# Graph sums of four blocks by row gathers on GpSimd, GpSimd's arithmetic moved to VectorE and DMA, main part unrolled

## The reference

```python
xn = _layernorm(x)
# graph part
h = xn * rsqrt(max(deg_out, 1))[:, None]
agg = segment_sum(h[src], dst, num_segments=N)
g = relu((agg * rsqrt(max(deg_in, 1))[:, None]) @ W + b)
g = g / max(norm(g), 1e-12)
# linear attention, 8 heads of 64, no softmax
dots = einsum('bnd,bnhe', instance_norm(k), instance_norm(v))
mix = ((q @ dots) / N) @ w_out.T + b_out
x = x + g + mix
# mixture of 8 experts, each token to its best one, with a capacity
return x + ffn(_layernorm(x))
```

## Time and profile before

| | before |
|---|---|
| median of 3 runs | 1471.17 us (1469.41 to 1475.35) |
| span of the profiled execution | 1429.1 us |
| that execution's own time | not listed; its span is 42.1 us below the median |
| PE busy | 1337.7 us (94%) |
| DVE busy | 1248.9 us (87%) |
| ACT busy | 962.9 us (67%) |
| POOL busy | 648.8 us (45%) |

### The profile page before, as it was taken

The page is one execution under the profiler, slowest core; times in us unless marked ns, Lnnn a source line. Parts: engine busy times, 40 slices in busy tenths (PEclk is TensorE's granted clock), DMA queues, the critical chain, the costliest instruction groups (busy, mean ns, idle before and its releaser), DMA issues. The chain is left out here.

```text
span 1429.1 us, 43152 instructions
## 1 busy us (share of the span) xinstructions
PE 1337.7 (94%) x14715; PEld 1128.4 (79%) x14717; DVE 1248.9 (87%) x2315; ACT 962.9 (67%) x2239; POOL 648.8 (45%) x645
## 2 busy tenths in 40 slices
PE   4899999958999999999999999999998999899987
PEld 3466666637899999999999999999995788889986
DVE  7899999988789999999999999999976586867786
ACT  5588888775567767677677677676663658464754
POOL 4557663062234433334433344333331676776574
PEclk9899999988999999999999999999999999999999
DMA  9211111000011111121111121111113443353220
GB/s 299 60 42 46 54 45 39 23 31 1 4 62 50 37 37 37 37 72 38 37 37 37 37 73 37 37 37 37 41 71 104 129 139 107 102 161 95 76 77 26
DMA packets 61264, 89.57 MB, mean 63 GB/s; under 512 B 10231, under 2 KB 40591, under 8 KB 61154
## 3 DMA queue, kind: packets, MB, share of 16 engines
q1 hardware_dynamic: 50032, 67.20, 13.9%
q0 software_dynamic: 11136, 21.23, 5.3%
HBM read 62.91 MB, written 34.49 MB: 68 GB/s over the span
## 5 line engine op out<-in xcount | busy, mean ns | idle before, releaser
L1621 PE MATMUL bank<-reg_b,reg_a 128*128 128x256 f16 x4802 | 642.7, 273 | 0.7 <-ACT reg_a L1206 0.7
L1206 ACT ACTIVATE reg_a<-bank 128x392 f16<-128x392 f32 x784 | 358.8, 499 | 159.2 <-PE bank L1613 154.3
L1621 PEld LDWEIGHTS bank<-reg_b,reg_a 128*128 128x128 f16 x4802 | 428.9, 97 | 42.7 <-issue 0.9
L1860 DVE TENSOR_TENSOR reg_c<-iota_v,reg_c 128x2048 f16<-128x2048 f16 (+1 forms) x298 | 432.2, 1465 | 21.6 <-PE bank L1613 11.2
L845 POOL COPY key_deg<-deg_k 128x1 f32 (+1 forms) x49 | 105.0, 2143 | 463.0 <-DVE reg_c L1989 463.0
L1613 PE MATMUL bank<-reg_a,reg_c 128*128 128x98 f16 x3136 | 261.4, 208 | 6.1 <-DVE reg_e L2069 2.2
L1613 PEld LDWEIGHTS bank<-reg_a,reg_c 128*128 128x128 f16 x3136 | 213.5, 98 | 24.9 <-issue 7.9
L1860 DVE TENSOR_TENSOR reg_a<-iota_h,reg_c 128x1568 f16<-128x1568 f16 x196 | 215.7, 1101 | 0.0
L1816 PE MATMUL bank<-w_hi,hid_hi 128*128 128x256 f32 (+1 forms) x368 | 107.3, 292 | 12.7 <-DVE w_lo L2342 7.5
L1818 PE MATMUL bank<-w_hi,hid_lo 128*128 128x256 f32 (+1 forms) x368 | 104.6, 284 | 0.0
L1817 PE MATMUL bank<-w_lo,hid_hi 128*128 128x256 f32 (+1 forms) x368 | 104.5, 284 | 0.0
(11 more groups left out here) (360 smaller groups left out, 2529.4 us busy)
## 6 DMA issues: line engine op xcount, KB each, us to landing
reg_b<-in_L_ffn_w SPq DMA_DIRECT2D x16, 1024.0 KB
tok_rows<-reg_e SPq DMA_DIRECT2D x24, 512.0 KB, 3.8
x_t<-in_x SPq DMA_DIRECT2D x24, 256.0 KB
xnT_t<-xnT_rows SPq DMA_DIRECT2D x24, 256.0 KB, 2.9
out<-reg_e SPq DMA_DIRECT2D x24, 256.0 KB
xnT_rows<-xnT_t SPq DMA_DIRECT2D x13, 256.0 KB, 2.0
reg_a<-in_x SPq DMA_DIRECT2D x1, 3072.0 KB, 24.1
xnT_rows<-mix_hl SPq DMA_DIRECT2D x12, 256.0 KB, 2.0
```

The source lines that it names most:

```text
L1206: return a.activation(AT[k].rearrange("p h (w t) -> p h w t", w=2)[:, :, :, s * GROUP:(s + 1) * GROUP], tile_ps[bk][:, 0:GROUP * 2 * NB].r ...
L1621: ins = t_.matmul(agg_ps[k][:, 0:D], AT[k][:, h, :], h_all[:, h, half * D:(half + 1) * D], start=(first and h + half == 0), stop=(last and ...
L1860: return v_.tensor_tensor(out.rearrange("p t (v u) -> p t v u", u=2), iota.rearrange("p (v u) -> p v u", u=2).unsqueeze(1).to_broadcast(sh ...
```

## The change

- Blocks 14, 15, 30 and 31 (pairs 7 and 15, `GATHERED`) get no marks, builds and matmuls. h is written to DRAM in f32 (`h_rows`): seven DMAs write the high half, seven add the low half. Then POOL issues 56 row gathers (`GROUNDS`) for each of the four blocks: each takes one row of h for each of the 128 destination nodes and adds it in an accumulator in SBUF, two accumulators a block. DVE makes the row numbers (`gather_rows`; absent edges point to a row of zeros) and adds and scales the accumulators (`gathered`). Where a gathered block has an in-degree above 56, the branch with rounds is taken.
- POOL's arithmetic in the main part is gone: the keys are made on DVE alone (`keys`); the sum's scaling by ACT and POOL is one DVE operation out of PSUM (`scaled`); gnn_b is added on DVE (`biased`); x + b_out is made in DRAM (`x_bias`): SP copies x there in the start, and POOL adds b_out with one accumulating DMA.
- The 45 blocks that are left keep their order. From the fourth on they are straight code in each engine's `sparse`. Finishes still take 32 slots, and start at slots 48, 80, 112, 144, 176, 208, 240, and from pair 7 on every 28 slots: 268, 296 and so on to 688. Pair 7's gathered sums are needed at slot 268, pair 15's at 492. The last finish ends at slot 720.
- h is stored as [half][tile][feature] instead of [tile][half][feature].

```diff
+GATHERED = (7, 15)
+GB = 2 * len(GATHERED)
+GROUNDS = 56
+GACC = 2
+GSPACE = 28
...
+def finish_starts():
+    starts = []
+    for q in range(NQ - 1):
+        ready = 0 if q in GATHERED else (AT_POS[2 * q + 1] + 2) * SLOTS
+        starts.append(max([ready] + [s + GSPACE for s in starts[-1:]]))
+    assert all(s % CG == 0 for s in starts)
+    assert starts[NQ - 2] + 2 * SLOTS == len(DENSE) * SLOTS
+    return starts
...
         sp.dma_start(wq[:, :, :], wv[:, 0:IC, :]).then_inc(w_in2, 16)
+        sp.dma_start(x_bias.rearrange("(p j) d -> p (j d)", p=XB_ROWS), x.rearrange("(p j) d -> p (j d)", p=XB_ROWS)
+                     ).then_inc(xb_in, 16)
         sp.dma_start(gate_w_sb[:, :, :], gate_w.rearrange("(c p) d -> p c d", p=P)).then_inc(w_in2, 16)
...
-        pool.wait_ge(degin_set, 3)
-        block_keys(0, 0)
+        pool.wait_ge(xb_in, 16)
+        g.dma_start(x_bias[:, :], b_out.rearrange("(a d) -> a d", a=1).to_broadcast([N, D]), accum_op=ALU.add
+                    ).then_inc(xb_set, 16)
         pool.wait_ge(deg_ok, 1)
         pool.wait_ge(hw_out, H_POOL[-1] + 1)
-        h_part(H_POOL[:6])
-        block_keys(1, 1)
-        h_part(H_POOL[6:])
+        h_part(H_POOL)
...
-            pool.wait_ge(fin_pool, q + 1)
-            apart(pool)
-            g.tensor_tensor(gs, gs, gnn_b_bc[:, :].unsqueeze(1).to_broadcast([P, w, D]), ALU.add
-                            ).then_inc(fin_scaled, 2)
...
+            rows = h_rows.rearrange("(p t) d -> p t d", t=NB)
+            pool.wait_ge(h_pool, len(H_POOL))
+            pool.wait_ge(h_lo, 14)
+            for n, t0 in enumerate(HG * i for i in H_GROUPS):
+                if n == 2:
+                    pool.wait_ge(h_lo, 26)
+                if n == 4:
+                    pool.wait_ge(h_lo, N_LATE)
+                g.dma_start(out=rows[:, t0:t0 + HG, :], in_=h_all[:, 0, t0:t0 + HG, :]).then_inc(h_stored, 16)
+            pool.wait_ge(h_stored, 16 * NB // HG)
+            for t0 in (HG * i for i in H_GROUPS):
+                g.dma_start(out=rows[:, t0:t0 + HG, :], in_=h_all[:, 1, t0:t0 + HG, :], accum_op=ALU.add
+                            ).then_inc(h_stored, 16)
+            pool.wait_ge(h_stored, 2 * 16 * NB // HG)
+            landed = [[[0] * GACC for m in range(2)] for _ in range(2)]
+            for i, q in enumerate(GATHERED):
+                pool.wait_ge(idx_set, i + 1)
+                if i >= 2:
+                    pool.wait_ge(acc_out, 2 * i - 2)
+                for j in range(GROUNDS):
+                    for m in range(2):
+                        k = j % GACC
+                        if j >= GACC:
+                            pool.wait_ge(acc_in[i % 2][m][k], 16 * landed[i % 2][m][k])
+                        at = bass.IndirectOffsetOnAxis(ap=slot_src[:, 2 * q + m, j:j + 1], axis=0)
+                        if j < GACC:
+                            ins = g.indirect_dma_start(out=acc[i % 2][m][k], out_offset=None, in_=h_rows, in_offset=at)
+                        else:
+                            ins = g.indirect_dma_start(out=acc[i % 2][m][k], out_offset=None, in_=h_rows, in_offset=at,
+                                                       compute_op=ALU.add)
+                        ins.then_inc(acc_in[i % 2][m][k], 16)
+                        landed[i % 2][m][k] += 1
...
-        def key_halves(b):
+        def keys(b, k, n=None):
             apart(dve)
             src_b = slot_src[:, ds(b, 1), :].rearrange("p a j -> p (a j)")
             v_.tensor_scalar(key_i[:, 0, :], src_b, P - 1, None, ALU.bitwise_and)
             v_.tensor_scalar(key_i[:, 1, :], src_b, 7, None, ALU.logical_shift_right).then_inc(key_int, 1)
+            dve.wait_ge(key_int, (b if n is None else n) + 1)
+            apart(dve)
+            v_.scalar_tensor_tensor(key_t[k][:, 0, :], iota_k[:, :], deg_k[:, ds(b, 1)], key_i[:, 0, :], ALU.subtract, ALU.max)
+            v_.tensor_copy(key_t[k][:, 1, :], key_i[:, 1, :]).then_inc(key_set, 1)
...
+        def scaled(b, k, n=None, gs=g_s):
+            out_ = last_fin.g[:, 0, :] if fixed(b, NB - 1) else gs[:, k, :]
+            dve.wait_ge(agg_done, (b if n is None else n) + 1)
+            apart(dve)
+            v_.scalar_tensor_tensor(out_, agg_ps[k][:, 0:D], rin[:, ds(b, 1)], norm_bc[:, :], ALU.mult, ALU.mult
+                                    ).then_inc(agg_out, 1)
...
+        def gathered(i, q, gs):
+            added = []
+            for m in range(2):
+                for k in range(GACC):
+                    dve.wait_ge(acc_in[i % 2][m][k], 16 * (GROUNDS // GACC) * (i // 2 + 1))
+                for k in range(1, GACC):
+                    ins = v_.tensor_tensor(acc[i % 2][m][0], acc[i % 2][m][0], acc[i % 2][m][k], ALU.add)
+                added.append(sparse_step(ins))
+            for m in range(2):
+                dve.wait_ge(sparse_dve, added[m])
+                v_.scalar_tensor_tensor(gs[:, m, :], acc[i % 2][m][0], rin[:, 2 * q + m:2 * q + m + 1], norm_bc[:, :],
+                                        ALU.mult, ALU.mult).then_inc(acc_out, 1)
...
+                def fin(c):
+                    if c == 0:
+                        of = DENSE[p - 2]
+                        dve.wait_ge(fin_relu, before[of // 2] + 1)
+                        scaled(of, of % 2, b - 2, gs_of[of // 2])
+                    if c == 2 and p - 3 < len(GATHERED):
+                        gather_rows(GATHERED[p - 3])
+                    for q, at in active(p, c * CG):
+                        if q in GATHERED:
+                            done = (acc_out, 2 * GATHERED.index(q) + 2)
+                        else:
+                            done = (agg_out, AT_POS[2 * q + 1] + GB + 3)
+                        if at == 0 and q in GATHERED:
+                            dve.wait_ge(fin_relu, before[q] + 1)
+                            gathered(GATHERED.index(q), q, gs_of[q])
+                        if at < SLOTS:
+                            first(q, at // CG, (gs_of[q], done))
+                        else:
+                            second(q, at // CG - CHUNKS, True)
+
+                gnn(b, p % 2, fin, False, DENSE[p + 2] if p + 2 < len(DENSE) else None)
```

More of the change, by code:

```diff
@@ L467, in build, with places_of, active, main_phase @@
     XG = [(0, 4), (4, 20), (24, 24)]
-    def main_phase(eng, gnn, prepare, first, second, tail, ahead=None):
+    starts = finish_starts()
+    gs_of = [g_s if q in (0, NQ - 2, NQ - 1) or q % 2 == 0 else g_alt for q in range(NQ)]
+    Places = namedtuple("Places", "count route place late")
+    KEYS_AT = 2
+    def places_of(q):
+        keys_at = (KEYS_AT - starts[q]) % SLOTS
+        return Places(8 if keys_at == 6 else 5, 2 if keys_at == 6 else 1, 16 if keys_at == 14 else 14, keys_at == 14)
+    def active(p, s):
+        at = p * SLOTS + s
+        return [(q, at - starts[q]) for q in range(NQ - 1) if 0 <= at - starts[q] < 2 * SLOTS]
+    def main_phase(eng, gnn, prepare, first, second, tail, sparse, ahead=None):
         def blocks(with_rounds):
@@ L499, in main_phase @@
         with eng.Else():
-            pairs(False)
+            if ahead:
+                ahead()
+                blocks(False)
+            sparse()
         tail()
@@ L512, in kv_phase, with finish_slot @@
             late_pair(i, i % 2)
+    def finish_slot(first, second, p, s):
+        for q, at in active(p, s):
+            if at < SLOTS:
+                first(q, at)
+            else:
+                second(q, at - SLOTS)
     def first_pair(q):
@@ L1233, in gnn @@
                 act.wait_ge(deg_ok, 2)
-            if not fixed(b, 0) and not fixed(b, 1):
-                agg_evac(b - 2, k)
             for s in range(SLOTS):
@@ L2133, in prepare @@
         def prepare(b, c):
+            if (b, c) == (2, 0):
+                scaled(0, 0)
             if (b, c) == (1, 1):
@@ L2149, in prepare, with first @@
                                         ).then_inc(mix_prep, 1)
-        def first(q, c):
+        def first(q, c, sums=None):
             w, o = blocks_of(q), fin_of(q)
+            if c == 0 and not sums:
+                scaled(q * 2 + 1, 1)
             if c == 1:
+                biased(q, *(sums or ()))
+            if c == (places_of(q).route if sums else 1):
                 n[0] = 0
@@ L2160, in first @@
             if c == 3:
-                if not first_pair(q) and not fixed(q, NQ):
+                if not first_pair(q) and not fixed(q, NQ) and not (sums and places_of(q).late):
                     add_slots(q - 1)
@@ L2208, in second @@
                 ins.then_inc(fin_xn2, 1)
+                if sparse and places_of(q).late and q > 0:
+                    add_slots(q - 1)
             if c == 1:
```

317 lines of the change are left out of this document (189 added, 128 removed).

## The result

The changed kernel is slower: 1528.6 us (median of 4) against 1470.3 in the first measurement, ratio 1.0396 (95% interval 1.0366 to 1.0426), and 1485.5 against 1431.5 in a second one, ratio 1.0393 (1.0364 to 1.0423). The forecast was 1426, with a range from 1408 to 1467.

A forecast was written before the change was run, and what follows sets the result against it. It took the graph sums to be PE-bound with DVE close behind; terms A to G summed to -44.8 us, span 1429.1 to 1384.3, plus 42.1 around it: 1426 us, range 1408 to 1467 for 8 in 10.

The forecast's parts named there:

- Part A: Main part: four blocks leave PE, 700.8 us become 645.3, so -55.5 us, the term on which everything stands.
- Part B: Main part: DVE takes over POOL's work, 27.2 us against PE's 27.0 per 28 slots, a tie; +6 us.
- R4: Rival, main part: marks do not get faster although POOL's arithmetic is gone; 54 us more, 1480 us; chance 0.05.
- Part C: Gathered pairs: DVE's additions and scalings cost 1.85 us a pair, +3.7 for both, 0 if DVE isn't the later engine.
- Part D: Start: the copy of x from DRAM to DRAM on SP's queue costs +4 us, bounds 0 and +20.
- Part E: Turn to the main part: POOL's half of h earlier, -1.5 us; the addition of b_out in DRAM costs 0.
- R2: Rival, turn to main part: POOL held by the addition in DRAM until it lands, first sums 40 us late; 1466 us; chance 0.07.
- Part F: Gathered pairs: gathers start at 385 us, take 1.5 us a step and end 28 us early; cost 0, beginning above 1.75.
- R1: Rival, gathered pairs: POOL's issues wait behind DVE's marks all the time, PE waits about 155 us; 1581 us; chance 0.08.
- Part G: End: POOL no longer disturbs DVE and the last block's sum is scaled once; -1.5 us, bounds -3 and 0.
- The frame: Whole kernel: the 42.1 us between the profiled span and the median of 1471.17 were put around the new span too.
- signs of being wrong: PE idle before first sums or at about 581 us behind a DMA, steps above 1.75, or PE waiting over 1 us for marks.

The follow-up runs named there:

- e3: The changed kernel without the copy of x and the addition of b_out, all 224 gathers writing instead of adding; 1400.0 us, ratio 0.9788 to the kernel before.
- e4: The changed kernel without the copy of x and the addition of b_out, 40 adding gathers a block instead of 56; 1398.4 us, ratio 0.9781.
- e8: The changed kernel with no pair gathered, x loaded from the input and b_out added in SBUF by DMA; ratio 1.0056 to the kernel before.
- e2: The changed kernel with neither the copy of x nor the addition of b_out, x loaded from the input; 1441.7 us, ratio 1.0073.
- e1: The changed kernel without the addition of b_out to the copy of x in DRAM; 1451.3 us, ratio 1.0138 to the kernel before.
- e13: The changed kernel, full result, its adding DMA reading b_out from the 128-partition copy in SBUF instead of one DRAM row; ratio 1.0101.
- e6: The changed kernel, full result, x loaded from the input and b_out added to it in SBUF by one POOL-issued DMA per pair; ratio 1.041.
- e10: The changed kernel with b_out written to the copy of x instead of added; only the key/value phase is read, the write landed after 102.5 us.
- e12: The changed kernel, its adding DMA reading x in 6250 rows of 1 KB instead of b_out; only key/value phase read, landing after 49.9 us.
- e11: The changed kernel, its adding DMA reading x in 5-KB rows instead of b_out; only key/value phase read, landing after 38.3 us.

## Why the prediction was wrong, point by point

- **Part A, four blocks off PE: right.** Blocks 3 to the last take 661.5 us without the two losses, against 704.9: -43.4, where A, B and C together were forecast at -45.8. e3 and e4, in which no gather is waited for, show -43 directly, again with B and C in it.
- **Part B: half the cost, and another picture.** B was forecast at +6, with DVE and PE in a tie at 28 slots and nothing lost at 32. DVE is below that: 539 of 600 us in e8, with pairs 32 slots apart (forecast 29.4 of 30.5 us), and 234.1 of 250 in e4 with pairs 28 apart. What costs is one wait of PE per pair on DVE's late norm (0.4 us of the 0.68), and it falls on all 23 pairs, those 32 slots apart too: e8 loses 12.1 us over blocks 3 to the last (less than 23 x 0.68, since the first pair's two blocks took 33.7 us before and take 31.3 there). That B and C together were forecast at +9.7 and came to +12.1 (-43.4 and A's 55.5) is luck: B was too small, and C's part hardly came. R4 is refuted: marks of 1214 ns.
- **Part C: right in its bounds.** In e3 and e4 the two blocks at the second gathered pair take 31.5 us, where the two of the same place in the next round of seven blocks take 31.1. So the cost is at most 0.4 us a pair, near the lower bound of 0, and not the 1.85 taken.
- **Part D, the copy: +4 forecast, 7.7 in the trace (1.1 of it also in e2, which has no copy) and 10 by e1 against e2.** Within its bounds.
- **Part E: the step that failed most.** The prediction put "0" for the addition, since it asked only when x is needed (378 us) and not what else uses the DMA engines until then. Measured +45.8 behind 269 us, of which the addition is 41 to 43 (the first builds of e1 and of the changed kernel, and e13). The rest is the turn itself, forecast at -1.5: from the key/value pair at 282 us to the first build, the versions without any addition in DRAM (e2 to e4, e6 to e8) take 1.2 to 3.5 us longer than the kernel before. Two errors are in the 0 for the addition. The price: 77 to 116 us from src_pad's rate came near the 118 measured, by luck, since the reason is the one source row. And the cover, which is the step that failed: the transfer lies beside the stores of the key/value phase, on which each pair waits two pairs later. The rival R2 had this transfer as well, but held up POOL with it (POOL was free after 4.3 us), and not the stores. The Trainium skill, "Collectives: The Full Stack", section "The bandwidth ceiling: the fold count and why AG ≠ RS ≠ AR", says that an add needs two source reads and so runs at about half a copy's rate. This transfer does not bear it out: writing took 102.5 us where adding took 111 to 118; but with one source row for all, it was held back by something else.
- **Part F: the start right by luck, the step wrong.** Gathers began at 437.1, 61.8 us behind the first build; forecast were 63 (385 against 322), and 384.1 is measured in e6, without the shift. But the forecast took them to wait for h in DRAM, and h had landed by 418.6, 43.3 us behind the first build. What they waited for are DVE's row numbers, which the prediction put into slack at 0 without asking when they come. So 18 of the 25 us by which the first pair came late lay idle here. The step was taken at 1.5 us from issues that only write; it is 2.12, since adding costs 1.54 at the least. 112 x 2.12 = 237 us end 25 us late. The text named 1.75 as the point where it begins. The cost was 44.6 us (29.1 and 15.5). R1's mechanism, issues held up beside DVE's marks, is small: at most 0.28 us of a step. The Trainium skill, "SBUF — State Buffer", section "SBUF: two separate sides", says that DVE and GpSimd share a port pair which one operation holds until it ends while the other is blocked, an operation with two inputs in SBUF only against GpSimd's reads. The trace agrees in kind: the 19 adding issues of the changed kernel without any DVE operation beside them took 1.54 us, the 31 beside marks alone 1.81, and one beside six marks and a 128x512 operation in an unbroken row 5.16. A wait for a whole mark at each gather did not occur.
- **Part G: -1.5 forecast, -0.8 measured** for tail and experts.
- **The frame:** the 42.1 us around the span mixed two chips. It shifted the absolute number, not the sign: the sum of terms was -44.8, the trace shows +54.0, and D, E and F are off by 3.7, 47.3 and 44.6 us, B and C by 2.4, G and blocks 0 to 2 by 0.8. Of the signs of being wrong that the prediction named, two came: PE idle with a DMA behind it at the first gathered pair, and steps above 1.75 us. For the stores it had none.

## What to carry to other kernels

A transfer is not free because its result is needed late: list every small store and load that shares the DMA engines with it while it runs, and how many buffers of slack each has. Price each form of an instruction by that form: a gather that adds is another instruction than one that writes, and where no row shows it the bound must reach to the deadline, here 1.75 us, which then decides the forecast. Ask of every input of a long list of DMAs when it is made, the small ones too: here the row numbers came 18 us behind the data. And set a profile's span against runs of the same chip before anything is added to it.

## What the runs showed of the hardware

- A DMA of 6250 rows of 1 KB into DRAM, all read from one kilobyte of DRAM, lands after 102.5 (write, e10) and 111.5 to 118.4 us (add); from 6250 different places after 49.9 us (e12), in 5-KB rows after 38.3 (e11), and from SBUF after 40.9 us for 6144 rows (e13).
- While the 118.4-us transfer runs, 256-KB stores of another queue land after 22 us instead of 2.0.
- An indirect DMA that adds costs GpSimd 1.54 us of issue while the other engines stand still and 1.81 on average beside them; one that writes costs 0.95 at the least and 1.24 on average (e3). 0.30 lie between two in both.
- GpSimd's indirect DMAs leave VectorE's 128x2048 marks at 1214 ns, its arithmetic stretches them to 1485 on average.
